# The last tile's rank part: from twelve plain products to seven combined ones, in a fused adapter and feed-forward kernel on one core

## The reference, cut to what matters

```python
def _L1_ffn_ref(x, base_W, router_W, lora_A, lora_B):
    base = jnp.einsum('bsd,od->bso', x, base_W)
    logits = jnp.einsum('bsd,ed->bse', x, router_W)
    ...
    mid = jnp.einsum('bsd,edr->bser', x, lora_A)
    mid = mid * w_dense[..., None]
    inc = jnp.einsum('bser,erd->bsd', mid, lora_B)
    return base + inc * SCALING
...
x = x + _L0_ffn_ref(_L0_cond_ref(x, ...), ...)
x = x + _L1_ffn_ref(_L1_cond_ref(x, ...), ...)
```

## Time and profile before

| | us |
|---|---|
| median of three runs | 902.22 |
| the three runs | 901.51, 902.22, 912.92 |
| the profiled execution's own time | 901.23 |
| its span, first to last instruction | 899.5 |
| PE busy in the span | 893.7 (99%) |
| PE weight loads | 782.0 |
| DVE busy | 673.8 (75%) |
| ACT busy | 326.7 (36%) |
| POOL busy | 147.3 (16%) |

### The profile page before, as it was taken

The page is one execution under the profiler, slowest core; times in us unless marked ns, Lnnn a source line. Parts: engine busy times, 40 slices in busy tenths (PEclk is TensorE's granted clock), DMA queues, the critical chain, the costliest instruction groups (busy, mean ns, idle before and its releaser), DMA issues.

```text
span 899.5 us, 13649 instructions
## 1 busy us (share of the span) xinstructions
PE 893.7 (99%) x4646; PEld 782.0 (87%) x4646; DVE 673.8 (75%) x1473; ACT 326.7 (36%) x545; POOL 147.3 (16%) x298
## 2 busy tenths in 40 slices
PE   9999999999999999999999999999999999999998
PEld 8999998888998888888888888888888888888887
DVE  6899899866587968888676677767766767767764
ACT  6578778411334423233322222222222222222220
POOL 0100010111002001414212312302302202302300
PEclk9999999999999999999999999999999999999999
DMA  9523330765412042575786887887887887886885
GB/s 360 194 83 114 121 126 25 255 217 170 143 51 95 0 141 100 186 264 199 230 300 245 295 296 256 285 293 251 287 304 247 288 292 257 284 300 243 293 276 195
DMA packets 60979, 192.52 MB, mean 214 GB/s; under 512 B 7761, under 2 KB 10730, under 8 KB 58990
## 3 DMA queue, kind: packets, MB, share of 16 engines
q1 hardware_dynamic: 50188, 160.04, 49.5%
q0 software_dynamic: 10432, 31.35, 11.8%
q10 hardware_dynamic: 290, 0.26, 0.1%
HBM read 159.39 MB, written 32.76 MB: 214 GB/s over the span
## 4 chain that ended last, share of the span: by engine, by line
PE 96%; DMA 3%; DVE 1%; ACT 0%; SPq 0%; issue 0%; DVEq 0%
PE bank L900 29%; PE bank L554 15%; PE bank L555 15%; PE bank L556 15%; PE bank L882 6%; PE bank L868 4%; PE bank L877 2%; PE bank L701 2%; DMA t_lo<-t_scratch 2%; PE bank L991 2%; DMA m_raw<-m1t 1%; PE bank L811 1%; PE bank L615 1%; PE bank L828 0%; PE bank L826 0%; PE bank L574 0%
## 5 line engine op out<-in xcount | busy, mean ns | idle before, releaser
L900 PE MATMUL bank<-g_hi,xs 128*128 128x512 f32 x448 | 152.6, 398 | 0.0
L525 POOL DMA_DIRECT2D p1sel<-p_scratch x128 | 65.6, 512 | 339.8 <-issue 339.7
L900 PE MATMUL bank<-t_hi,xs 128*128 128x512 f32 x328 | 109.2, 393 | 0.6 <-DMA t_lo<-t_scratch 0.6
L900 PEld LDWEIGHTS bank<-g_hi,xs 128*128 128x128 f32 x448 | 83.2, 188 | 15.7
L900 PE MATMUL bank<-g_lo,xs 128*128 128x512 f32 x224 | 88.4, 394 | 0.0
L1422 DVE TENSOR_TENSOR xs<-x_raw,xs 128x1024 fp32r<-128x1024 f32 x60 | 72.4, 1230 | 11.9 <-ACT xs L1068 11.9
L554 PE MATMUL bank<-gx,xs 128*128 128x304 f32 x256 | 78.3, 306 | 0.0
L556 PE MATMUL bank<-gx,xs 128*128 128x304 f32 x256 | 77.5, 303 | 0.0
L555 PE MATMUL bank<-gx,xs 128*128 128x304 f32 x256 | 77.4, 302 | 0.0
L900 PEld LDWEIGHTS bank<-t_hi,xs 128*128 128x128 f32 x328 | 61.6, 188 | 15.0 <-DMA t_lo<-t_scratch 2.0
L1068 ACT ACTIVATE xs<-x_raw 128x1024 fp32r<-128x1024 f32 x60 | 61.8, 1054 | 33.9 <-PE bank L900 33.2
(11 more groups left out here) (398 smaller groups left out, 2135.9 us busy)
## 6 DMA issues: line engine op xcount, KB each, us to landing
t_hi<-t_scratch SPq DMA_DIRECT2D x82, 512.0 KB, 5.4
t_lo<-t_scratch SPq DMA_DIRECT2D x82, 512.0 KB, 6.5
x_raw<-xq SPq DMA_DIRECT2D x16, 1024.0 KB, 6.9
out<-ost SPq DMA_DIRECT2D x62, 256.0 KB, 6.0
p1sel<-p_scratch POOLq DMA_DIRECT2D x64, 192.0 KB, 4.5
w_raw<-wall SPq DMA_DIRECT2D x16, 512.0 KB, 4.5
w<-e_scratch SPq DMA_DIRECT2D x6, 1024.0 KB, 5.1
ea<-e_scratch POOLq DMA_DIRECT2D x8, 644.0 KB, 4.4
```

Of the source, the lines that this page charges most:

```text
L525: pool.dma_start(f(p1sel[b][STK * s:STK * s + STK, cs]), p1_dram[bass.ds(i * STK, STK), cs]).then_inc(sems[b], 16)
L900: mm = nc.tensor.matmul(bk[j][:], l[:, c, :], m[:, c, :], start=first and c + k == 0, stop=c + k == KH + 1, skip_group_check=True)
```

## The change

The last tile's rank part takes the same seven-product form as in the tiles before it. `m0_terms` is called for bank 0 alone, behind product 12, in every tile. The sums for s1 to s4 are made in the last tile too, on ACT and DVE. The low terms of banks 2, 1, 0 come behind the turn of `mid`, and that of bank 3 opens `xb[:, 0, :]`. The seventh rank product `s3 * k3` is made in two halves of 256 columns, which open the two destinations that product 72 then adds to, and after it come five rank products (`last_ranks`), with a wait of PE on `x6_ok` in front of the last one. `t_loaded(0, 2)` and `t_loaded(1, 2)` keep their place in the text, ahead of the branch in which all this now stands. DVE gets a new closing sequence. The store and the reload of `p0`'s right half go. The core of the diff:

```diff
-            sp.wait_ge(g_lo_s, O_ALL)
-            for k, p in enumerate((p0_hi, p0_lo)):
-                sp.dma_start(p0_dram[k], f(p[:, 512:D])).then_inc(st_p0, 16)
...
-                elif tau + 2 == NT2:
-                    sp.wait_ge(s_lo_s, 2 * (NT2 - REG))
-                    sp.wait_ge(st_p0, 48)
-                    for k in range(2):
-                        sp.dma_start(f(p0r[:, k, :]), p0_dram[k]).then_inc(ld_p0, 16)
...
-                mm = product(12, 0, quarter(0, 0, 0), g_quarter(0, 0), True)
-                if tau + 1 < NT2:
-                    mm = m0_terms(0)
-                mm.then_inc(p1_mm, 1)
+                product(12, 0, quarter(0, 0, 0), g_quarter(0, 0), True)
+                m0_terms(0).then_inc(p1_mm, 1)
...
-                if last:
-                    m0_terms(2, True)
...
-                if last:
-                    pe.wait_ge(ld_p0, 48)
-                    m0_terms(1, True, None, p0_right)
...
                     low_term(2)
-                    m0_terms(3, True, xb[:, 0, :], p0_right)
-                    low_term(3, xb[:, 0, :])
                     low_term(1)
-                    m0_terms(0)
                     low_term(0)
-                    mid_ready(tau)
-                    mid_terms((2,))
-                    mid_terms((3,), xb[:, 0, :])
-                    mid_terms((1, 0))
+                    low_term(3, xb[:, 0, :], True).then_inc(low_mm, 1)
 
                 pe.wait_ge(u4_ok, n + 1)
                 t_loaded(0, 2)
...
                 else:
                     t_loaded(1, 2)
                     x_q = quarter(1, 1, 0)
-                    for q in range(2):
-                        qs = slice(256 * q, 256 * q + 256)
-                        dst = bk[3][:, qs] if q else xb[:, 1, qs]
+                    parts = [(xb[:, 1, 0:256], slice(0, 256)), (bk[3][:, 256:512], slice(256, 512))]
+                    pe.wait_ge(rs_hi_s, 2 * n + 1)
+                    pe.wait_ge(rs_lo_s, 2 * n + 1)
+                    for dst, qs in parts:
+                        mm = rank_product(dst, (s3_hi, s3_lo), (k3_hi[:, qs], k3_lo[:, qs]), qs.start == 0)
+                    mm.then_inc(rank_mm, 1)
+                    mid_ready(tau)
+                    last_ranks(tau)
+                    for dst, qs in parts:
                         for c in range(KH):
...
+            def last_ranks(tau):
+                n = tau - REG
+                rank_product(bk[0][:], mid[0], lbl).then_inc(rank_mm, 1)
+                rank_product(bk[2][:], mid[1], (k4_hi[:], k4_lo[:])).then_inc(rank_mm, 1)
+                pe.wait_ge(rs_hi_s, 2 * n + 2)
+                pe.wait_ge(rs_lo_s, 2 * n + 2)
+                pe.wait_ge(ev[1], tau)
+                pe.wait_ge(ev[3], tau)
+                rank_product(bk[4][:], s2, (k2_hi, k2_lo), True).then_inc(rank_mm, 1)
+                rank_product(bk[1][:], s4, lbr).then_inc(rank_mm, 1)
+                pe.wait_ge(x6_ok, n + 1)
+                rank_product(bk[4][:], s1, (k1_hi[:], k1_lo[:])).then_inc(rank_mm, 1)
...
-            v.wait_ge(out_mm, 4 * REG + 1)
-            nc.vector.tensor_tensor(p5_sum[:], bk[2][:], p5_sum[:], ALU.add).then_inc(fin_ok, 1)
-            v.wait_ge(out_mm, 4 * REG + 2)
+            v.wait_ge(low_mm, NT2)
             for q, part in enumerate((u4_sum, p1_sum)):
                 qs = slice(256 * q, 256 * q + 256)
-                nc.vector.tensor_tensor(p1_sum[:, qs], xb[:, 0, qs], part[:, qs], ALU.add).then_inc(fin_ok, 1)
-            v.wait_ge(out_mm, 4 * REG + 3)
-            out_sum(NT2 - 1, 1, bk[1], u4_sum)
+                tt(p1_sum[:, qs], xb[:, 0, qs], part[:, qs], ALU.add).then_inc(fin_ok, 1)
+            v.wait_ge(rank_mm, NR * n + L6)
+            tt(p5_sum[:], bk[4][:], p5_sum[:], ALU.add).then_inc(x6_ok, 1)
+            v.wait_ge(x6_ok, n + 1)
+            tt(p5_sum[:], bk[2][:], p5_sum[:], ALU.add).then_inc(fin_ok, 1)
+            v.wait_ge(rank_mm, NR * n + L3)
+            tt(u4_sum[:], bk[1][:], u4_sum[:], ALU.add).then_inc(b1_ok, 1)
+            v.wait_ge(rank_mm, NR * n + L5)
+            v.wait_ge(b1_ok, n + 1)
+            out_sum(NT2 - 1, 1, bk[4], u4_sum)
             v.wait_ge(fin_ok, 3)
+            tt(p1_sum[:], bk[4][:], p1_sum[:], ALU.add).then_inc(fin_ok, 1)
+            v.wait_ge(fin_ok, 4)
```

More of the change, by code:

```diff
@@ L36 @@
 R7, R6, R4, R2, R3, R5, NR = 1, 2, 3, 4, 5, 6, 6
+L2, L4, L6, L3, L5 = 2, 3, 4, 5, 6
 STK = 3 * RK
@@ L871, in plain_products, with m0_terms @@
                 mm.then_inc(g_all, 1)
-            def m0_terms(j, first=False, to=None, right=(p0_hi[:, 512:D], p0_lo[:, 512:D])):
+            def m0_terms(j):
                 b, h = j // 2, j % 2
-                hi, lo = right if h else (p0_hi[:, 0:512], p0_lo[:, 0:512])
-                for k, (l, m) in enumerate(((m0t_hi, hi), (m0t_hi, lo), (m0t_lo, hi))):
-                    mm = nc.tensor.matmul(bk[j][:] if to is None else to, vt(l, b), m, start=first and k == 0, stop=k == 2, skip_group_check=True)
+                hs = slice(h * 512, h * 512 + 512)
+                for k, (l, m) in enumerate(((m0t_hi, p0_hi), (m0t_hi, p0_lo), (m0t_lo, p0_hi))):
+                    mm = nc.tensor.matmul(bk[j][:], vt(l, b), m[:, hs], start=False, stop=k == 2, skip_group_check=True)
                 return mm
@@ L934, in winograd_products @@
                 product(36, 0, quarter(0, 0, 1), g_quarter(1, 0), False)
-                last = tau + 1 == NT2
-                p0_right = (p0r[:, 0, :], p0r[:, 1, :])
                 pe.wait_ge(ev[2], tau)
-                if last:
-                    m0_terms(2, True)
                 t_loaded(0, 1)
-                product(48, 2, quarter(0, 1, 1), (t_hi, t_lo), not last, lambda: t_loaded(1, 1)).then_inc(t_free, 1)
+                product(48, 2, quarter(0, 1, 1), (t_hi, t_lo), True, lambda: t_loaded(1, 1)).then_inc(t_free, 1)
                 pe.wait_ge(b1_ok if n else ev[1], n or tau)
-                if last:
-                    pe.wait_ge(ld_p0, 48)
-                    m0_terms(1, True, None, p0_right)
-                product(60, 1, quarter(1, 0, 1), g_quarter(1, 1), not last)
+                product(60, 1, quarter(1, 0, 1), g_quarter(1, 1), True)
                 mid_turn(tau)
@@ L979, in winograd_products, with low_term @@
                     x_q = quarter(1, 1, 0)
-                    for q in range(2):
-                        qs = slice(256 * q, 256 * q + 256)
-                        dst = bk[3][:, qs] if q else xb[:, 1, qs]
+                    parts = [(xb[:, 1, 0:256], slice(0, 256)), (bk[3][:, 256:512], slice(256, 512))]
[7 more added lines that the diff above has]
+                    for dst, qs in parts:
                         for c in range(KH):
                             for k, (l, m) in enumerate(((x_q[0], t_hi), (x_q[0], t_lo), (x_q[1], t_hi))):
-                                mm = nc.tensor.matmul(dst, l[:, c, :], m[:, c, qs], start=q + c + k == 0,
+                                mm = nc.tensor.matmul(dst, l[:, c, :], m[:, c, qs], start=False,
                                                       stop=c + k == KH + 1, skip_group_check=True)
                         mm.then_inc(fin_mm, 1)
-            def low_term(j, to=None):
+            def low_term(j, to=None, first=False):
                 b, h = j // 2, j % 2
-                return nc.tensor.matmul(bk[j][:] if to is None else to, vt(lowt, b), p1sel[b][:, h * 512:h * 512 + 512], start=False, stop=True,
+                return nc.tensor.matmul(bk[j][:] if to is None else to, vt(lowt, b), p1sel[b][:, h * 512:h * 512 + 512], start=first, stop=True,
                                         skip_group_check=True)
@@ L1011, in mid_ready @@
                     pe.wait_ge(af_lo_s, 3)
+            s2, s1, s4 = ((srk_hi[:, k, :], srk_lo[k][:]) for k in range(3))
+            mid = [(vt(midt_hi, b), vt(midt_lo, b)) for b in range(2)]
+            lbl, lbr = ((lb1_hi[:, hs], lb1_lo[:, hs]) for hs in halves)
+            def last_ranks(tau):
[10 more added lines that the diff above has]
+                rank_product(bk[4][:], s1, (k1_hi[:], k1_lo[:])).then_inc(rank_mm, 1)
             def rank_products(tau):
                 n = tau - REG
-                s2, s1, s4 = ((srk_hi[:, k, :], srk_lo[k][:]) for k in range(3))
-                mid = [(vt(midt_hi, b), vt(midt_lo, b)) for b in range(2)]
-                lbl, lbr = ((lb1_hi[:, hs], lb1_lo[:, hs]) for hs in halves)
                 pe.wait_ge(rs_hi_s, 2 * n + 2)
@@ L1031, in rank_products, with mid_terms @@
                 rank_product(bk[4][:], s1, (k1_hi[:], k1_lo[:])).then_inc(rank_mm, 1)
-            def mid_terms(banks=(3, 0, 2, 1), to=None):
-                for j in banks:
+            def mid_terms():
+                for j in (3, 0, 2, 1):
                     b, h = j // 2, j % 2
                     hs = slice(h * 512, h * 512 + 512)
-                    dst = bk[j][:] if to is None else to
+                    dst = bk[j][:]
```

(22 more changed lines are left out.)

11 lines of the change are left out of this document (4 added, 7 removed).

## The result

| | before | with the change |
|---|---|---|
| median, us | 901.56 (22 runs) | 904.85 (22 runs) |
| lowest to highest | 900.3 to 912.92 | 902.31 to 917.14 |
| profiled execution, own time / span | 901.23 / 899.5 | 903.41 / 901.7 |

The ratio is 1.003, with a 95% interval of 1.0016 to 1.0045: the change makes the kernel 0.3% slower, 3.3 us by the medians. The forecast was 906.0 us in a range of 903.0 to 909.0.

The account below looks back on a forecast made before the run. PE's order was taken as the time: -0.68 matmuls, +3.3 load wait, +0.1 restart and +0.3 `x6_ok` gave +3.0 us, with the clock 4.4. On 901.23 plus 0.4 for the median: 906.0 us, range 903.0 to 909.0.

Parts of the forecast that it names:

- The load's new wait: Last tile, in front of `s3 * k3`: PE arrives at 888.28 and waits 3.3 us for product 72's load, until 891.6.
- the rival in which it lands with most of its bytes: PE goes on at 890.0, the wait is 1.7 us, sum +1.4, 902.6 us; chance 6%.
- The restart: First matmul behind the load's wait takes 0.33 us to the next start instead of 0.23; cost 0.1 us.
- `x6_ok`: PE's wait for DVE's addition in front of the last rank product; cost 0.3 us.
- The 0.68 us of matmuls: Last tile's rank part: PE's matmuls go from 6.50 to 5.82 us, gain 0.68 us.
- The rank sums: DVE's sums in the last tile end at 890.6, inside the load's wait; cost nothing, 0.2 us if that wait weren't there.
- the +3.0 us without the clock: Whole change at full clock: -0.68 matmuls, +3.3 load, +0.1 restart, +0.3 `x6_ok`.
- The clock: PE's granted clock falls in the load's wait or shortly behind it; cost 1.4 us, between 0 and 2.8.
- a rival (it stays): The load's wait comes but the clock doesn't fall: +3.0, 904.2 to 905 us; chance 20%.
- The case I gave 58%: The forecast case: the load's wait comes and the clock falls, 904.8 to 907.5 us.
- The clock that stays low to the end: All 7.1 us of matmuls behind the load's wait take twice that: +3.0 + 7.1, 911.3 us; chance 10%.
- The removed traffic: Store and reload of `p0` go, 1 MB and four issues of SP: gain 0, at most 0.6 us.

Follow-up runs that it names:

- e1: Changed kernel with the wait for the load of `t_hi` and `t_lo` moved from in front of `s3 * k3` to in front of product 72; 901.55 us, ratio 1.0003.
- e3: Kernel before, with the load's wait (and `u4_ok`) moved from in front of product 72 to behind the first low term; 906.04 us, ratio 1.0052.
- e4: Changed kernel with the load's wait (and `u4_ok`) moved still earlier, ahead of the four low terms; 906.69 us, ratio 1.0071.
- e7: The changed kernel measured once more, nothing altered; 905.02 us, ratio 1.005.
- e2: Changed kernel plus 10 matmuls of 512 columns with unused result between the low terms and the load's wait; 903.38 us, ratio 1.0035.
- e5: e1 with the last rank product `s1 * k1` moved behind the first three matmuls of product 72; 900.81 us, ratio 0.9989.
- e6: e1 with the store and reload of `p0`'s right half put back; 901.30 us, ratio 1.0019.
- e8: e4 plus 12 matmuls of 512 columns with unused result in front of its wait; 904.45 us, ratio 1.0047.
- second run of e5: The kernel of e5 measured once more, nothing altered; 901.11 us, ratio 1.0007.

## Why the prediction was right

**The load's new wait** was the step that decided, and it is shown from three sides: taken out (e1) the loss goes, put into the kernel before (e3) it comes, moved further (e4) it grows. Its place, its start and the unmoved issues were as forecast. Its end was not: 891.02 instead of 891.6. The term had 3.3 us, of which 0.8 depended on one landing: 6.6 us in the trace of before, 5.8 in that of after. Over eleven traces the last transfer lands 5.8, 5.8, 5.8 and 6.0 us after its issue in the changed kernel, e7, e4 and e2, and 6.4 to 6.6 in before, e1, e3, e5, e6, e8 and the second run of e5. The difference lies in the last bytes. From 890.0 to 890.5 and from 890.5 to 891.0 the transfers' share was 0.25 and 0.10 before; with the change (same columns) it is 0.26 and 0.00:

```profile
890.00:890.50 0.50, 0.00 (x0) 0.00 (x0) 0.50 (x3) 0.00 (x0) 0.00 (x0) 1.00 0.26 98
890.50:891.00 0.50, 0.00 (x0) 0.01 (x1) 0.50 (x3) 0.00 (x0) 0.00 (x0) 1.00 0.00 0
```

Why this tail is shorter in some traces stays open. The landing at 890.82 puts the load between the forecast (891.5) and the rival in which it lands with most of its bytes (890.0).

**The matmuls and the small waits.** From the restart to product 72 I had 0.1 + 0.72 + 3.48 + 0.3 = 4.6 us; measured 4.61. The restart cost 0.08 us (0.20 to the second matmul, at a half-width pace of 0.12), for 0.1. `x6_ok` cost 0.24 us in front of its matmul (894.36 to 894.83, less a pace) and 0.11 behind it (894.83 to 895.17), for 0.3. From the landing to the restart it took 0.20 us, for 0.06. The 0.68 us of matmuls are in the turn: by its row in the changed kernel's trace the first low term starts at 887.33, forecast 887.26. The rank sums cost nothing, being inside the wait, and 0.33 us in e1, where 0.2 was forecast.

**The sum.** The last matmul starts 2.49 us later than before, with 3.0 forecast. The profiled execution as a whole lost 2.2 us, because the span ended 3.33 us behind that start instead of 3.62. The length behind the last issue of an output differed by 0.3 us (2.22 after 899.48, 2.52 before); I had put it as unchanged. So the +3.0 us without the clock came out 0.8 us too high: 0.5 in PE's path, nearly all of it the load's landing, and 0.3 at the end.

**The clock** was in the forecast (it falls) and in a rival (it stays), and both happen. Of the changed kernel's 20 undisturbed runs, 7 have a granted clock of 1.000 and a median of 903.76 us, 9 have 0.998 and 905.00, and 4 have 0.996 and 906.48. The fall thus cost 1.2 us in the nine and 2.7 us in the four; the forecast had 1.4, with 2.8 as the upper end. That 1.4 comes so near is partly luck: it was the middle between nothing and 2.8, and no row stood behind it. The 2.8 were half of 5.6 us at the low clock; the low stretch is 3.4 us long in e7 and in e3. In e7 it begins before the restart (890.0 to 893.4), as forecast, and in e3 0.9 us behind it. No trace holds one of the executions at 0.996, so what happens in them stays open. The case I gave 58% came in 13 of 20 executions (and in all five of e7), the one I gave 20% in seven, and the median of the mixture, 904.85, lies at the lower edge of the first case's 904.8 to 907.5. The clock that stays low to the end, +7.1 us, never came. The Trainium skill says ("TensorE: Matmul & The Clock Gate", "HAM oscillation — how this bites in real kernels") that waits for DMAs between bursts of matmuls bring the clock down. e7 agrees, and so do e2 and e8 from the other side: the same waits, filled, leave the clock at 1.00.

**The base.** The 906.0 us were the profiled execution's 901.23 us, the sum of 4.4 and 0.4 more for the median. The median of 22 runs, 901.56, with the same sum gives 906.0 as well. Measured were 904.85, 1.1 us less: 0.5 us are PE's path (2.49 for 3.0), 0.3 the shorter end in the profile, and the remaining 0.3 us would be the seven executions without a fall, which isn't shown by itself.

**The removed traffic** was put at 0, and nothing in e6 speaks against it.

## What to carry to other kernels

A block of work between the issue of a load and its wait is also the cover of that load: before it is moved or shortened, look at the margin at the wait (1.6 us here, with 5 us of cover), and move the wait along with the first instruction that reads the data, not with the text around it. When the trace names one releaser for a wait on several semaphores, compare the landings of the transfers among them too. And a wait of TensorE costs more than its length in those executions where the clock falls in it; if it can't be avoided, matmuls whose result isn't used can be cheaper than idle time.

## What the runs showed of the hardware

The granted clock fell in an idle time of TensorE of only 2.5 us (e7, some 2 us into it), and it can fall when the engine is already at work again (e3, 0.9 us behind a wait of 3.2 us). In both it was low for 3.4 us. Whether it falls at a wait of this length differs from execution to execution of the same kernel: 13 of 20 in the changed kernel and five of five in e7; it was below 0.999 in all nine undisturbed runs of e4, with 3.4 us in its trace. Four transfers of 512 KB, issued within 1.7 us and alone on the queues, take 7.5 us from the first issue to the last landing in the changed kernel's trace (883.30 to 890.82) and 8.3 us in that of before, with nearly the same work around them.
